# Out-projection of an attention layer: one f32 product replaced by three f16 products of split operands

## The reference

```python
q = (x @ wq).reshape(b, s, H, QH).transpose(0, 2, 1, 3)
...
attn = jax.nn.softmax(scores, axis=-1)
out = jnp.einsum('bhqk,bhkd->bhqd', attn, v)
out = out.transpose(0, 2, 1, 3).reshape(b, s, H * VD)
return out @ wo
...
x = x + _layernorm(attention(_layernorm(x)))
x = x + _layernorm(moe(_layernorm(x)))
```

## Time and profile before

| | |
|---|---|
| median of 3 runs | 1389.68 us |
| lowest and highest | 1383.07 and 1397.15 us |
| the profiled execution's own time | 1384.21 us |
| its span, first to last instruction | 1382.4 us |
| mean granted clock of TensorE | 0.948 |
| PE busy, share of the span | 1195.3 us, 86% |
| DVE busy | 818.0 us, 59% |
| ACT busy | 802.6 us, 58% |
| POOL busy | 734.6 us, 53% |

### The profile page before, as it was taken

The page is one execution under the profiler, slowest core; times in us unless marked ns, Lnnn a source line. Parts: engine busy times, 40 slices in busy tenths (PEclk is TensorE's granted clock), DMA queues, the critical chain, the costliest instruction groups (busy, mean ns, idle before and its releaser), DMA issues. The chain is left out here.

```text
span 1382.4 us, 20149 instructions
## 1 busy us (share of the span) xinstructions
PE 1195.3 (86%) x6860; PEld 580.9 (42%) x6861; DVE 818.0 (59%) x1830; ACT 802.6 (58%) x1242; POOL 734.6 (53%) x444
## 2 busy tenths in 40 slices
PE   4998898998998899989999889999999998578820
PEld 3533446443443633333333543333333335466610
DVE  6555666565567755565555765666556515565546
ACT  3634653665564465656565457777777785256632
POOL 0055440564563266646565537877778785235545
PEclk9988999999999999999999999999999999799975
DMA  9046200110011010000010101000000000146754
GB/s 282 19 103 134 54 1 1 49 28 16 23 39 31 1 47 16 16 16 16 14 34 8 32 12 54 18 7 23 24 23 13 12 23 16 55 132 193 182 130 133
DMA packets 63032, 70.28 MB, mean 51 GB/s; under 512 B 10080, under 2 KB 52448, under 8 KB 62816
## 3 DMA queue, kind: packets, MB, share of 16 engines
q1 hardware_dynamic: 56656, 56.26, 14.6%
q0 software_dynamic: 4864, 10.51, 3.3%
q10 hardware_dynamic: 1424, 2.38, 0.7%
HBM read 37.50 MB, written 14.83 MB: 38 GB/s over the span
## 5 line engine op out<-in xcount | busy, mean ns | idle before, releaser
L547 POOL TENSOR_TENSOR D<-D,B 128x1024 f32<-128x1024 f32 (+3 forms) x256 | 512.9, 2004 | 177.6 <-ACT B L733 160.7
L1078 DVE TENSOR_REDUCE mxp<-ps 128x1 f32<-128x512 f32 (+3 forms) x640 | 385.8, 610 | 311.1 <-PE ps L1585 214.9
L733 ACT ACTIVATE B<-ps 128x1024 f32<-128x1024 f32 (+1 forms) x320 | 286.1, 894 | 239.5 <-PE ps L1611 167.1
L1629 PE MATMUL ps<-B,kv 128*64 128x512 f32 (+3 forms) x1280 | 305.2, 557 | 11.8 <-ACT C L626 10.9
L626 ACT ACTIVATE ps<-D 128x1024 f32<-128x1024 f32 (+1 forms) x320 | 287.6, 899 | 27.3 <-DVE D L1094 16.9
L1611 PE MATMUL ps<-A,KTh 128*128 128x512 f16 (+3 forms) x768 | 209.1, 355 | 4.7 <-ACT ps L626 4.7
L540 POOL TENSOR_TENSOR D<-B 128x1024 f32<-128x1024 f32 (+1 forms) x32 | 71.0, 2218 | 211.5 <-ACT B L733 211.5
L1585 PE MATMUL ps<-KTh,A 128*128 128x512 f16 (+3 forms) x384 | 136.8, 359 | 3.2 <-DVE mxp L1078 3.0
L1611 PE MATMUL ps<-A,KTl 128*128 128x512 f16 (+3 forms) x384 | 135.8, 354 | 0.0
L1629 PEld LDWEIGHTS ps<-B,kv 128*64 128x64 f32 x1280 | 63.9, 135 | 103.1 <-issue 75.7
L1611 PEld LDWEIGHTS ps<-A,KTh 128*128 128x128 f16 x768 | 63.4, 98 | 102.6 <-issue 55.4
(11 more groups left out here) (264 smaller groups left out, 1831.5 us busy)
## 6 DMA issues: line engine op xcount, KB each, us to landing
results<-B SPq DMA_DIRECT2D x64, 128.0 KB
xnTl<-in_L_ffn_experts_gate_up SPq DMA_DIRECT2D x16, 256.0 KB, 2.8
A<-in_L_attn_wq SPq DMA_DIRECT2D x4, 768.0 KB, 20.7
B<-in_L_attn_x SPq DMA_DIRECT2D x5, 512.0 KB, 6.0
D<-in_L_attn_wo SPq DMA_DIRECT2D x2, 1024.0 KB, 21.0
A<-C SPq DMA_DIRECT2D x16, 128.0 KB, 2.4
A<-C SPq DMA_DIRECT2D x32, 64.0 KB, 2.0
A<-stg SPq DMA_DIRECT2D x16, 128.0 KB, 2.3
```

The source lines that it names most:

```text
L547: nc.gpsimd.tensor_tensor(acc[:, :, c0:], acc[:, :, c0:], Pr[:, kt % P_RING, :, c0:], ALU.add).then_inc(sum_done, 1)
L733: nc.scalar.activation(Pr[:, kt % P_RING, :, c0:], ps[:, 2 * (kt % ST_RING):2 * (kt % ST_RING) + 2, c0:], ACT.Exp, scale=SM_SCALE).then_in ...
L1078: V.tensor_reduce(mxp[:, s, i4, kc:kc + 1], ps[:, BK_X + j % MX_RING, 0:w], AX.X, ALU.max).then_inc(mx_free, 1)
L1629: ins = T.matmul(ps[LORA * s:LORA * (s + 1), BK_O, c0:], kv[:, kt, 0:LORA], Pr[:, kt % P_RING, s, c0:], start=(kt == 0), stop=(kt == KT - 1))
```

## The change

The folded weights are kept as two f16 tiles, `WOh` and `WOl`, scaled by 64 (`WS`), and the turned attention output as two f16 halves in the same bytes as before. The product of a tile becomes 24 f16 products by the helper `three`. The low part of the weights is a new DVE instruction for each head; the low part of the turned output is `turned_low(j)`, two new DVE instructions for each tile, and PE now waits for these (`ontl_ready`) both ahead of the product and ahead of overwriting banks 6 and 7.

```diff
-        WO = sb("WO", [P, NP, E])
+        WOh = sb("WOh", [P, NP, E], F16)
+        WOl = sb("WOl", [P, NP, E], F16)
...
-        OnT_A = A[:, 3072:5120].rearrange("p (r n c) -> p r n c", r=2, n=NP)
+        OnT_A = A[:, 3072:5120].bitcast(F16).rearrange("p (r u n c) -> p r u n c", r=2, u=2, n=NP)
...
-                    copy(WO[o:o + LORA, g // 2, :], ps[o:o + LORA, 6 + g % 2, 128:384])
+                    copy(WOh[o:o + LORA, g // 2, :], ps[o:o + LORA, 6 + g % 2, 128:384], WS)
...
                         act.wait_ge(t2_ready, (qc * TC + j) * 2 + b + 1)
-                        copy(OnT[:, j % 2, 4 * b:4 * b + 4, :],
+                        if j >= 2:
+
+                            act.wait_ge(mo_ready, qc * TC + j - 1)
+                        copy(OnT[:, j % 2, 0, 4 * b:4 * b + 4, :],
                              ps[:, 6 + b, :].rearrange("p (n q) -> p n q", n=4)).then_inc(ont_ready, 1)
...
-                    copy((ysb3 if qc == NC - 1 else yb)[:, j, :], ps[:, j % 2, 0:E]).then_inc(ysb_ready, 1)
+                    copy((ysb3 if qc == NC - 1 else yb)[:, j, :], ps[:, j % 2, 0:E], 1 / WS).then_inc(ysb_ready, 1)
...
             for g in range(H):
                 dve.wait_ge(wfh_done, g + 1)
+                o = LORA * (g % 2)
+                V.scalar_tensor_tensor(out=WOl[o:o + LORA, g // 2, :], in0=ps[o:o + LORA, 6 + g % 2, 128:384], scalar=WS,
+                                       in1=WOh[o:o + LORA, g // 2, :], op0=ALU.mult, op1=ALU.subtract)
...
+            def turned_low(qc, j):
+
+                for b in range(2):
+                    dve.wait_ge(ont_ready, (qc * TC + j) * 2 + b + 1)
+                    V.tensor_tensor(OnT_of(qc)[:, j % 2, 1, 4 * b:4 * b + 4, :],
+                                    ps[:, 6 + b, :].rearrange("p (n q) -> p n q", n=4),
+                                    OnT_of(qc)[:, j % 2, 0, 4 * b:4 * b + 4, :], ALU.subtract).then_inc(ontl_ready, 1)
...
                 normalised(qc, 0)
                 normalised(qc, 1)
+                turned_low(qc, 0)
                 if qc:
                     for part in range(1, 4):
                         places(qc - 1, part, 2)
                     shares(qc - 1, 0)
                     shares(qc - 1, 1)
                 for j in range(TC):
+                    if j + 1 < TC:
+                        turned_low(qc, j + 1)
                     if j + 2 < TC:
                         normalised(qc, j + 2)
                     first_norm(qc, j)
...
                         if j:
-                            pe.wait_ge(ont_ready, (qc * TC + j - 1) * 2 + b + 1)
+                            pe.wait_ge(ontl_ready, (qc * TC + j - 1) * 2 + b + 1)
...
-                    pe.wait_ge(ont_ready, (qc * TC + j + 1) * 2)
+                    pe.wait_ge(ontl_ready, (qc * TC + j + 1) * 2)
...
                     for n in range(NP):
-                        ins = T.matmul(ps[:, j % 2, 0:E], OnT_of(qc)[:, j % 2, n, :], WO[:, n, :],
-                                       start=(n == 0), stop=(n == NP - 1))
+                        ins = three(ps[:, j % 2, 0:E], OnT_of(qc)[:, j % 2, 0, n, :], OnT_of(qc)[:, j % 2, 1, n, :],
+                                    WOh[:, n, :], WOl[:, n, :], n == 0, n == NP - 1)
```

More of the change, by code:

```diff
@@ L140, in attention_moe @@
         On_A = A[:, 1024:3072].rearrange("p (r c) -> p r c", r=2)
-        OnT_A = A[:, 3072:5120].rearrange("p (r n c) -> p r n c", r=2, n=NP)
+        OnT_A = A[:, 3072:5120].bitcast(F16).rearrange("p (r u n c) -> p r u n c", r=2, u=2, n=NP)
         On_B = B[:, 0:2048].rearrange("p (r c) -> p r c", r=2)
-        OnT_B = B[:, 2048:4096].rearrange("p (r n c) -> p r n c", r=2, n=NP)
+        OnT_B = B[:, 2048:4096].bitcast(F16).rearrange("p (r u n c) -> p r u n c", r=2, u=2, n=NP)
         QT_A = A[:, :].bitcast(F16).rearrange("p (h w q) -> p h w q", h=H, w=2)
@@ L232, in attention_moe @@
         den_read, log_out = sem("den_read"), sem("log_out")
-        den_ready, t1_ready, on_ready, t2_ready, ont_ready, mo_ready, ysb_ready = map(sem, (
-            "den_ready", "t1_ready", "on_ready", "t2_ready", "ont_ready", "mo_ready", "ysb_ready"))
+        den_ready, t1_ready, on_ready, t2_ready, ont_ready, ontl_ready, mo_ready, ysb_ready = map(sem, (
+            "den_ready", "t1_ready", "on_ready", "t2_ready", "ont_ready", "ontl_ready", "mo_ready", "ysb_ready"))
         xr_in, xn2_ready, xt2_ready, x2h_done, x2l_done = map(sem, (
```

## The result

| | before | after |
|---|---|---|
| median, timed on one chip (4 runs each) | 1388.8 us | 1409.9 us |
| lowest and highest | 1383.1 and 1397.2 us | 1407.7 and 1415.6 us |
| the profiled execution's own time | 1384.2 us | 1409.7 us |
| its span | 1382.4 us | 1407.9 us |

The ratio is 1.0145, 95% interval 1.0108 to 1.0182: slower by a little over 1%, clear of the noise. The forecast was 1403 us with a range of 1390 to 1413.

What follows compares the result with a forecast made beforehand. PE and DVE were taken to arrive together at chunk ends, so a shorter product alone wins nothing. Ends 9.4, folding 2.7 and clock 1 gave +13.1 us on the median 1389.7: 1403 us, range 1390 to 1413.

Steps and rivals of the forecast that it cites:

- The products: Out-projection in chunk ends: 24 f16 instructions, 2.80 us a tile instead of 3.62, saving PE 13.1 us over 16 tiles.
- The weight loads: In the f16 products: loads of about 107 ns stay overlapped; the rival, weights not hidden, 1423 us, chance 0.02.
- The cost of `turned_low`: Chunk ends: 20.6 us new DVE work, lengthening the four ends by 9.4 us, the middle of 6.5 and 12.3.
- the clock: Chunk ends: PE rests more, so a lower granted clock adds 1 us, bounds 0 and 6.8.
- PE's rest ahead of the last product: Each chunk end: sign that PE is idle there, released by DVE's low part; the last two products no longer back to back.
- signs named for being wrong: Low parts under 0.5 us on DVE, products staying back to back, or ACT's three delays gone.
- The question that I left open: Ends of chunks 1 to 3: delays moving with instructions give +12.3 us over all ends, keeping their time +6.5.
- The folding: Folding of the weights: one new DVE instruction a head, 0.42 us, delays PE; +2.7 us, bounds 1.7 and 3.
- the clock falls: Rival, chunk ends: last product and first scores run at 1.2 GHz, +10.4 us instead of +1, 1412 us; chance 0.2.
- the bound of 1%: Whole kernel: within 1% is 1375.8 to 1403.6 us; chances faster 0.04, same 0.5, slower 0.46.

Runs made afterwards that it cites:

- e_low_on_pe: Changed kernel, variance moved ahead of head 1's low parts, turned output's low part made by PE and ACT, not DVE: 1414.4 us, ratio 1.0124.
- e_no_low: Changed kernel without DVE's low parts in the chunk ends, the third product reading the high part instead: 1402.9 us, ratio 1.0069 to the kernel before.
- r_after2: Changed kernel a third time, nothing edited: 1411.3 us, ratio 1.0116 to the kernel before.
- e_var_first: Changed kernel with DVE's variance of the latents moved ahead of head 1's low parts: 1414.3 us, ratio 1.0145 to the kernel before.
- e_no_low_vf: Changed kernel without DVE's low parts in the chunk ends and with the variance moved ahead of head 1's low parts: 1400.2 us, ratio 1.0022.
- the second trace of before: Kernel before once more, nothing edited: 1395.2 us, ratio 0.9983 to the other runs of the same kernel.

## Why the prediction came out as it did

**The products** were right where the clock is full: 24 instructions, the first three starting at 231.63, 231.74 and 231.85 us, 0.11 us apart, so 2.8 us. They were not where it is down, 4.1 to 5.2 us for two or three products of each trace. The weight loads stay hidden, as the earlier trace rows had it: their groups have means of 100 to 108 ns here, under a matmul's own step of 110 ns. The rule in the Trainium skill (TensorE: Matmul & The Clock Gate, "LDWEIGHTS (loading the stationary operand)"), the number of columns over 1.2, gives 107 ns for 128 columns, an estimate by that page; the trace agrees.

**The cost of `turned_low`** was right in length (681 to 683 ns an instruction) and in its place on DVE: chunk 0 is 2.2 us longer, forecast 2.2; chunk 2 is 1.8 to 3.1 us longer than the first trace before, forecast 1.3 to 2.9; chunk 3 is 2.5 to 4.4 longer, forecast 1.3 to 3.5. For chunk 1 the forecast was 1.7 to 3.7; against the first trace before it is 4.8 to 5.7, against the second nothing. The row it rested on, the copy of y at 476.27, was from an execution with short delays. With the means of the table the four ends cost 10.7 us, against 9.4 forecast and 1 for the clock. That the sums agree is luck in part: the delays fell elsewhere than in the trace that the forecast was made from, and the clock fell at the products. PE's rest ahead of the last product, released by DVE's low part, came as forecast in the first trace, 1.75, 2.26 and 3.24 us in chunks 0, 1 and 3; in the third trace the last two products of chunks 2 and 3 still ran back to back, one of the signs named for being wrong, since the one ahead took 5.1 and 5.2 us at the lower clock.

The question that I left open, whether ACT's delays move with their instructions or keep their time, has both answers in part. In chunks 2 and 3 of all twelve traces but that of e_low_on_pe, a delay of 3.4 to 5.7 us stands ahead of the same copy, that of y for tile 1. In chunk 3 it is 4.93 us when ACT is ready at 16.9 us into the end (kernel before), 5.58 when ready at 16.5 (e_no_low), and 3.86 when ready at 19.5 (r_after2): by and large, the later ACT comes, the less it waits.

**The folding** was the step that failed, together with **the clock**. The prediction had "+2.7 us, bounds 1.7 and 3" and took its price of the clock, "+1 us, bounds 0 and 6.8", from the ends of chunks alone. The part of the 2.7 that is DVE's own work was about right: where the clock holds (e_var_first, e_no_low_vf, whose variance waits for one low part less) the folding is 2.2 us longer than before. What was missed is that the 0.84 us by which heads 0 and 1 delay the variance would come out at PE as a rest of 1.30 us in place of 0.54, and that the clock would fall about a rest of that size, as it did in five traces of five: 43.4 us in the mean of three, another 6.2 us. I had the earlier trace rows side by side and drew the clock from the second only for places like the one it stood in. The rival "the clock falls", 1412 us, came near in its time. It had the ends alone, and there the products did meet the lower clock, in one to three ends of each trace and at tile 2 as much as at the last; the folding, where the clock cost 6.2 us, it didn't name.

**The rest.** Terms measured one at a time on the chip: weights' low part 0.49%, DVE's low parts 0.80%, f16 products with the 2.2 us that the weights' low parts keep in the folding about nothing (0.22%, interval from -0.11 to 0.54). 0.49 + 0.80 = 1.29%, some 18 us, against 16 to 20 us for the whole change. The forecast of 13.1 us was 3 to 7 short, and the 6.2 us of the clock in the folding are of that size. So 1409.9 lies at the upper edge of the forecast's own range of 1397 to 1410, and over the bound of 1% behind which the prediction put a chance of 0.46. The prediction was taken from a profiled execution 5.5 us under its median and corrected for that, rightly: the second trace of before, at 1393.7 us of span, has what the first lacked, 5.6 us in chunk 1 and 8.6 in the last stage.

**What stays open.** What ACT waits for in its delays, and DVE in the slow passage of the last stage. Both keep to the same instructions in kernels with different numbers of instructions ahead of them. In the two traces without the slow passage the gathers were issued over 41.1 and 41.0 us, in the others over 38.7 to 39.2; which of the two is the cause was not tried. No version of the change beats the kernel before: the best, with both costs taken out, is level with it.

## What to carry to other kernels

Before pricing a cheaper instruction, ask whose wait ends last where it stands: 10 us less PE work in the chunk ends bought nothing, and 20 us of extra DVE work in the same places, with the clock that it lowered, cost 11. Work added ahead of a short chain that PE waits for costs more than its own length when it stretches a rest of PE, since the granted clock may fall behind it: here sixteen instructions of 0.42 us cost 7 us. And one trace of a kernel is one draw: two traces of the same kernel before differed by 11 us, in places that a comparison would have blamed on the change.

## What the runs showed of the chip that was not expected

- The granted clock fell to half about a rest of PE of 1.30 us in a stretch in which it was otherwise busy, in five traces of five, and about one of 0.67 us in one of four, with two traces equal up to that instant going different ways.
- It fell at the out-projection too once the products were spaced by rests of 2 us and more: 4.34 and 4.44 us for the last two products of chunk 1 in place of 2.78.
- Once down in the folding, it stayed there for 14 to 17 us although PE was 100% busy in every stretch of 4 us from 46 to 58 us.
- ACT's delays ahead of one and the same instruction shrink when ACT comes later and grow when it comes earlier (3.86 to 5.72 us in chunk 3), so they take back what a faster product saves.
- DVE has a passage in the last stage in which instructions start about 2 us apart without a visible cause, in one execution of a kernel and not in another, worth 8 to 9 us.
